# Expert tiles in the order in which they fill, with the first weights fetched for each tile as TensorE's stationary operand, and a start phase with smaller plans

## The chip, the core and the metric

The kernel is one program on one core of a Trainium2 chip. The metric is the device time of one execution in microseconds (us). Three executions of the kernel before took 6120.17, 6154.52 and 6066.71 us, median 6120.17. Five engines run side by side, each with its own instruction stream, and meet only through semaphores: TensorE (PE, with its weight loads shown as PEld), VectorE (DVE), ScalarE (ACT), GpSimd (POOL) and SyncE (SP). A name with a q behind it (SPq, POOLq) is the engine's instruction queue, where DMAs are issued.

## What is computed

The reference is one layer of a graph network followed by a mixture of experts, for 6250 nodes of 256 numbers and 200000 edges.

```
h   = gat(layernorm(x), W1, 4 heads);  h = elu(h);  g = gat(h, W2, 1 head)
      # gat: h = x @ W; per edge e = leaky_relu(s[src] + d[dst]); softmax of e over
      # the edges of one dst (self loops added); out[dst] = sum of weight * h[src]; + b
x   = x + g
n   = layernorm(x)
p   = softmax(n @ gate_w + gate_b)          # 8 experts
top2_vals, top2_idx = top_k(p, 2)
out = x + sum over the two experts e of a node:
          p_e * (gelu(n @ W1[e] + b1[e]) @ W2[e] + b2[e])    # 256 -> 512 -> 256
```

Everything is float32.

## The kernel before

`build` runs the phases one behind the other, with a barrier between two of them. The 6250 nodes are NT = 49 tiles of 128.

1. `start_phase` (0 to 139 us) normalizes the 49 node tiles, multiplies each with W1 (and the attention vectors folded into it) and stores a table of rows in DRAM. Beside this it plans the edges: it counts how many windows of 128 edges fall to each node tile, ranks the tiles by that (`rank_tiles`), gives each item its tile (`place_items`), and brings 13 blocks of source and destination indices in. On DVE all this stands between the normalizing steps of the tiles, at fixed tile numbers (`COUNT_AT`, `RANK_AT`, `ITEMS_AT`, `BLOCK_AT`). ACT first issues the loads of the weights and twelve small loads of attention columns (L624), then takes part in the tiles.
2. `shift_phase` and `edge_phase`, once for each of the two graph layers. In `edge_phase` POOL gathers eight times 128 source rows per step (L1002), ACT and DVE make the weights, PE sums rows with a 0/1 matrix (L1149), and DVE adds the sums (L1257). In `shift_phase` POOL issues the first 16 gathers (L694) while DVE prepares bounds and multiplies all of `acc` with the weights `ws` of the self loops (L818).
3. `route_phase` (5394 to 5556): SP loads all weights of all experts into SBUF (L1480, L1481; W1 4 MB, W2 4 MB, biases 3 MB in copies for all partitions). DVE finds the two best experts of each node and a slot in a list sorted by expert. The list has SLOT_TILES = 106 tiles of 128 slots; each expert's part is filled up to whole tiles. POOL then scatters the 49 tiles of rows twice (L1502) into the DRAM list `sent`, all first choices and then all second ones; between the two, DVE writes the new home number into the rows (L1581), for which it waits until the first 49 scatters have landed.
4. `expert_phase` (from 5564) walks over the 106 tiles k in the order of the list. SP loads `xe` (L1622, two buffers). PE transposes it (`turn_x`, L1668), ACT copies it to SBUF (L1781), PE multiplies with W1 (`up`, L1678: x is the stationary operand, 512 columns of W1 move), DVE adds b1 (L1729), ACT applies gelu (L1785), PE transposes the four pieces of the result (`turn_h`, L1687), DVE copies them (L1736), PE multiplies with W2 (`down`, L1697), DVE adds b2 (L1743), POOL scatters the result into `back` (L1651). The order on PE is written out by hand: in step k stand up(k+1), turn_x(k+2), turn_h(k), down(k-1). SP's load of tile k waits until tile k-2 is transposed and its home numbers are read (L1620, L1621). The first expert tile begins when all scatters have landed.
5. `combine_phase` (from 6018) reads the two results of each node back (L1819), weighs and adds them.

A float32 matmul appears in the trace as two passes, each with a weight load. `steps(eng, count, body, ways, peeled)` writes out the first and last steps and puts a loop around the others.

## Time and profile before

| | us |
|---|---|
| median of 3 executions (lowest, highest) | 6120.17 (6066.71, 6154.52) |
| the profiled execution, its own time | 6092.53 |
| span of its trace | 6090.7 |
| busy: PE / DVE / POOL / ACT | 3576.1 / 3420.2 / 3368.1 / 1636.8 |
| start phase, until the first shift phase | 139 |
| the two edge phases | 2589 + 2594 |
| routing up to the first scatter, the scatters | 28, 134 |
| expert stage, combining | 462, 73 |

The profile is of one execution, so every duration below comes from it; its own time is 27.6 us under the median. Engine rows give the start, the busy time, the engine, the line of kernel.py and what is written from what; a bracket gives the idle time of the engine before it and what ended it. The granted clock (PEclk) is given as a share of TensorE's 2.4 GHz; 0.50 is the lower of its two levels, 1.2 GHz.

### The profile page before, as it was taken

To read this page: it belongs to the slowest core of one execution; us is meant where nothing else is said; L and a number is where in the kernel's file an instruction comes from. 1 tells how busy PE (TensorE), PEld (TensorE's weight loads), DVE (VectorE), ACT (ScalarE), POOL (GpSimd) and SP (SyncE) were. 2 spreads that over 40 slices of the span, in tenths; PEclk is the share of its full clock that TensorE was granted. 3 is DMA by queue.
4 is the path that set the end of the run, shared out by engine and by line. 5 is a ranking of instruction groups with operands and counts; after the bars stand their busy time and mean duration, and the time that the engine had idled before them with its cause. 6 is when DMAs were issued, how large, how long until landed. Compare 5 with 4: busy or idle time off the path is not lost. (4 is left out here: it accounts for less than half of the span.)

```text
span 6090.7 us, 75071 instructions
## 1 busy us (share of the span) xinstructions
PE 3576.1 (59%) x12549; PEld 2299.2 (38%) x12550; DVE 3420.2 (56%) x8873; ACT 1636.8 (27%) x3595; POOL 3368.1 (55%) x3575
## 2 busy tenths in 40 slices
PE   5455555565555555554556666566666656624994
PEld 3233333333333333332333333333333333312773
DVE  7555555555555555555555555555555555531444
ACT  3222222222222222221233332322233333311222
POOL 4655555555555555555555555555655555644222
PEclk8666667766777777776676666666666676667997
DMA  4344444444444444443444444444444444442224
GB/s 127 104 109 108 105 108 110 109 107 106 109 108 109 110 110 110 110 104 86 111 114 114 115 114 114 113 114 114 114 113 114 114 113 114 118 137 86 91 64 155
DMA packets 321285, 670.43 MB, mean 110 GB/s; under 512 B 76855, under 2 KB 152773, under 8 KB 320938
## 3 DMA queue, kind: packets, MB, share of 16 engines
q0 software_dynamic: 170848, 469.37, 29.3%
q1 hardware_dynamic: 148585, 199.90, 11.5%
q10 hardware_dynamic: 1792, 0.53, 0.0%
q8 instruction: 18, 0.29, 0.0%
q14 instruction: 42, 0.34, 0.0%
HBM read 602.38 MB, written 75.12 MB: 111 GB/s over the span
## 5 line engine op out<-in xcount | busy, mean ns | idle before, releaser
L1002 POOL DMA_INDIRECT rows<-table,idx x3200 | 3031.4, 947 | 2086.8 <-issue 925.9
L1149 PE MATMUL bank<-rows,hit 128*128 128x260 f32 (+1 forms) x6464 | 2655.5, 553 | 2049.4 <-DVE acc L1257 1033.4
L1149 PEld LDWEIGHTS bank<-rows,hit 128*128 128x128 f32 x6464 | 1538.6, 265 | 2916.4 <-issue 1406.1
L1257 DVE TENSOR_TENSOR acc<-acc,bank 128x260 f32 (+1 forms) x3232 | 1356.4, 420 | 1385.5 <-remote 569.6
L1032 ACT ACTIVATE arg<-arg 128x32 f32<-128x32 f32 (+1 forms) x404 | 88.4, 219 | 3415.3 <-DVE arg L1237 2364.4
L1244 DVE TENSOR_TENSOR rows<-rows,bank 128x1024 f32<-128x1024 f32 x808 | 946.0, 1212 | 11.1 <-issue 9.7
L1211 DVE TENSOR_TENSOR hit<-bank,dst_loc 128x256 f32<-128x256 f32 x1616 | 671.7, 417 | 69.9 <-issue 58.6
L1222 DVE TENSOR_REDUCE bank<-bank 128x64 f32<-128x192 f32 (+1 forms) x404 | 115.4, 286 | 667.5 <-remote 598.8
L1026 ACT ACTIVATE hit_t<-gap,ones 128x1024 bf16<-128x1024 bf16 x404 | 463.8, 1148 | 20.3
L1021 ACT ACTIVATE gap<-loc,minus_node 128x1024 bf16<-128x1024 bf16 x404 | 462.6, 1145 | 11.7 <-DMA loc<-loc_row 11.5
L1138 PE MATMUL bank<-du,hit_t 128*128 x3232 | 340.9, 182 | 129.9 <-issue 127.6
L1138 PEld LDWEIGHTS bank<-du,hit_t 128*128 128x128 bf16 x3232 | 271.4, 102 | 332.2 <-issue 245.6
L1651 POOL DMA_INDIRECT back<-ye,xe_home x106 | 101.9, 962 | 341.3 <-DVE xe_home L1752 336.2
L1678 PE MATMUL bank<-fw,xet 128*128 x424 | 200.7, 596 | 0.9 <-ACT xet L1781 0.8
L1697 PE MATMUL bank<-fw,hidt 128*128 x848 | 200.5, 379 | 0.0
L1781 ACT COPY xet<-bank 128x256 f32<-128x256 f32 x106 | 39.5, 373 | 461.9 <-PE bank L1668 461.9
L1697 PEld LDWEIGHTS bank<-fw,hidt 128*128 128x128 f32 x848 | 152.9, 190 | 16.7 <-issue 0.2
L1729 DVE TENSOR_TENSOR hid<-bank,fb 128x512 f32<-128x512 f32 x106 | 73.3, 691 | 119.9 <-PE bank L1678 119.9
L1668 PE MATMUL bank<-ident,xe 128*128 128x128 f32 x212 | 41.1, 276 | 155.5 <-DMA xe<-sent 155.5
L1502 POOL DMA_INDIRECT sent<-acc,slot x98 | 96.2, 982 | 60.2 <-issue 29.3
L1743 DVE TENSOR_TENSOR ye<-bank,fb 128x256 f32<-128x256 f32 x106 | 45.0, 424 | 123.6 <-PE bank L1697 123.6
L1668 PEld LDWEIGHTS bank<-ident,xe 128*128 128x128 f32 x212 | 29.9, 142 | 211.9 <-issue 211.1
(223 smaller groups left out, 2191.9 us busy)
## 6 DMA issues: line engine op xcount, KB each, us to landing
loc<-loc_row SPq DMA_DIRECT2D x404, 256.0 KB
rows<-table,idx POOLq DMA_INDIRECT x3200
sent<-zeros SPq DMA_DIRECT2D x202, 68.3 KB
xe<-sent SPq DMA_DIRECT2D x106, 128.5 KB
got<-back SPq DMA_DIRECT2D x96, 128.0 KB, 3.4
fw<-in_L_ffn_W SPq DMA_DIRECT2D x16, 512.0 KB, 9.0
table<-acc POOLq DMA_DIRECT2D x49, 130.0 KB
table<-acc SPq DMA_DIRECT2D x49, 128.5 KB
```

The source lines that it names most:

```text
L1002: pool.indirect_dma_start(rows[:, way, n, 0:R], None, table, bass.IndirectOffsetOnAxis(idx[:, way, n:n + 1], 0)).then_inc(rows_in[way], 16)
L1021: nc.scalar.activation(gap[:, :], loc[:, way % 2, :], ACT.Abs, bias=kp.minus_node[:, 0:1]).then_inc(gap_ready, 1)
L1026: nc.scalar.activation(hit_t[:, way % 2, :, :].rearrange("p n e -> p (n e)"), gap[:, :], ACT.Relu, bias=kp.ones[:, 0:1], scale=-1.0).then_ ...
L1138: last = nc.tensor.matmul(du_bank[:, n * 6 * H:(n + 1) * 6 * H], hit_t[:, way % 2, n, :], eb.du3[:, t, :, 0:2 * H], start=True, stop=True)
L1149: nc.tensor.matmul(sum_bank[n % 4][:, 0:R], hit[:, way, n, :], rows[:, way, n, 0:R], start=True, stop=True).then_inc(summed, 1)
L1211: nc.vector.tensor_tensor(hit[:, way, some, :], col.unsqueeze(1).to_broadcast([P, PAIR, P]), eb.dst_loc[:, bass.ds(s * ST + pair * PAIR, P ...
L1222: nc.vector.tensor_reduce(du_edge, spread_out, AX.X, ALU.add).then_inc(du_kept, 1)
L1244: nc.vector.tensor_tensor(r, r, weight[:, some, :].unsqueeze(3).to_broadcast([P, PIECE, H, D // H]), ALU.mult).then_inc(scaled, 1)
L1257: nc.vector.tensor_tensor(kp.acc[:, t, 0:R], kp.acc[:, t, 0:R], sum_bank[n % 4][:, 0:R], ALU.add).then_inc(added, 1)
L1651: pool.indirect_dma_start(kp.back, bass.IndirectOffsetOnAxis(home[:, way:way + 1], 0), ye[:, way % 2, :], None).then_inc(y_out[way % 2], 16)
L1678: last = nc.tensor.matmul(kp.bank[2 + j][:, :], xet[:, j, c * P:(c + 1) * P], fb.w1[:, e, c, :], start=(c == 0), stop=(c == 1))
L1697: last = nc.tensor.matmul(kp.bank[6 + j][:, 0:D], hidt[:, j, c * P:(c + 1) * P], fb.w2[:, e, c, :], start=(c == 0), stop=(c == HC - 1))
```

## The change

The change rewrites the start and everything behind the edge phases, which it leaves as they are.

**Experts.** `route_phase` and `expert_phase` become one block without a barrier between them.
- The tiles are worked in the order in which they fill up while the node tiles are sent. DVE computes for each list tile the node tile that completes it, ranks these keys (two small products on PE), and writes a table of expert numbers and first rows, `table_of`.
- POOL sends first and second choices in turns (the second one three tiles behind, behind a wait for the first one's landing), eight pairs ahead, and then one pair before each second result scatter. SP's load of tile k waits for the second send of node tile (k + 7) // 2.
- W2 stays resident. W1 does not: SP fetches W1 of the tile's expert, 512 KB, into one of four slots, two tiles ahead. The fetch waits until gelu has freed the slot.
- `up` uses W1 as stationary operand (8 products of 128 columns of x), so that the result comes out transposed. The four transposes, DVE's bias and DVE's copy go; gelu reads PSUM in four pieces with the bias as a column per partition, which DVE picks out (`pick_bias`).
- On PE step k is turn_x(k+2), up(k+1), down(k).

**Shift phases.** `ws` is in a PSUM bank instead of SBUF; the product over `acc` is the same.

**Start.** x is loaded in pairs of tiles with eight buffers; the attention vectors come as four loads of rows and are transposed by PE; ranking works on 49 partitions with rows of 49 instead of 128 partitions with 2401; items are placed with small products on PE; the addition of eps moves into ACT's square root; constants of the later phases are made here.

The diff, cut:

```diff
@@ build @@
-            fb.w1 = fb.sb("fw1", [P, EXPERTS, 2, HID], F32)
...
@@ start_phase @@
-    COUNT_AT, RANK_AT, ITEMS_AT = 2, 4, 6
-    BLOCK_AT = [8 + 3 * blk for blk in range(BLOCKS)]
+    TURN_2, COPY_2, FOLD_2, KEEP_2 = 1, 2, 3, 4
+    COUNT_AT, RANK_AT, ITEMS_AT = 3, 5, 9
+    BLOCK_AT = [12 + 35 * blk // 12 for blk in range(BLOCKS)]
+    XSETS = 8
...
-                    done.then_wait(tt(less[:, :, :], key[:, :].unsqueeze(1).to_broadcast([P, NT, NT]),
-                                      key[:, :].unsqueeze(2).to_broadcast([P, NT, NT]), ALU.is_lt))
+                    done.then_wait(ts(less[:, 0, :], key[:, 0:NT], key[:, NT:NT + 1], None, ALU.is_lt))
+                    done.then_wait(tt(less[:, 1, :], less[:, 0, :], length[:, 0:NT], ALU.mult))
...
+                    done.then_wait(ts(past[:, :], item_row[:, :], end[:, :], None, ALU.is_ge))
+                    nc.vector.scalar_tensor_tensor(within[:, :], item_row[:, :], rank[:, 1:2], past[:, :],
+                                                   ALU.is_ge, ALU.subtract).then_inc(within_ready, 1)
...
+                    for m, a in enumerate((a_src, a_dst)):
+                        act.dma_start(vec[n][m * H:(m + 1) * H, :], a).then_inc(att_in[n], 16)
@@ shift_phase @@
-        ws = b.sb(f"ws_{layer}", [P, NT, HEADS], F32)
+        ws = kp.bank[2][:, 0:NT * HEADS].rearrange("p (t h) -> p t h", t=NT)
@@ expert_phase, SP @@
+                def load_weights(k, way):
+                    e = sp.value_load(fb.table_of[0:1, bass.ds(k, 1)], min_val=0, max_val=X - 1)
+                    if not number(k) or k >= RING:
+                        sp.wait_ge(gelu_ready, (k - RING + 1) * HC)
+                    sp.dma_start(w1[:, way % RING, :, :], fw1[bass.ds(e, 1)].rearrange("o (c p) n -> p (o c) n", p=P)
+                                 ).then_inc(w1_in[way % RING], 16)
+
+                def load(k, way, turn):
+                    if not number(k) or k + 2 < T:
+                        load_weights(k + 2, way + 2)
+                    j, after = way % 2, (way + 7) // 2
+                    row = sp.value_load(fb.table_of[0:1, bass.ds(k + T, 1)], min_val=0, max_val=(T - 1) * P)
+                    if not early(k):
+                        sp.wait_ge(x_turned, k - 1)
+                        sp.wait_ge(home_ready, k - 1)
+                    if not number(k) or turn * 4 + after < NT:
+                        sp.wait_ge(second_sent[after % 4], (turn + after // 4 + 1) * 16)
+                    sp.dma_start(xe[:, j, :], kp.sent[bass.ds(row, P), :]).then_inc(x_in[j], 16)
...
@@ expert_phase, POOL @@
+                def send_second(t):
+                    few = LAST if t == NT - 1 else P
+                    pool.wait_ge(first_sent[t % SENDS], 16 * (t // SENDS + 1))
+                    nc.gpsimd.iota(kp.acc[:, t, D:D + 1], [[0, 1]], base=(SLOT_TILES + NT + t) * P, channel_multiplier=1,
+                                   allow_small_or_imprecise_dtypes=True).then_inc(home_moved, 1)
...
+                for t in range(SENDS):
+                    send_first(t)
+                for t in range(FIRST):
+                    send(t)
+                for k in range(T):
+                    if k % 2 == 0:
+                        send(k // 2 + FIRST)
+                    store(k)
@@ expert_phase, PE @@
+                def up(k, way, turn):
+                    j = way % 2
+                    pe.wait_ge(w1_in[way], (turn + 1) * 16)
+                    pe.wait_ge(xet_ready, k + 1)
+                    if not early(k):
+                        pe.wait_ge(gelu_ready, (k - 1) * HC)
+                    for h in range(HC):
+                        for c in range(2):
+                            last = nc.tensor.matmul(kp.bank[2 + j][:, h * P:(h + 1) * P],
+                                                    w1[:, way, c, h * P:(h + 1) * P], xet[:, j, c * P:(c + 1) * P],
+                                                    start=(c == 0), stop=(c == 1))
+                    last.then_inc(up_done, 1)
...
+                def step(k, way, turn):
+                    j = way % 2
+                    if not number(k) or k + 2 < T:
+                        turn_x(k + 2, j, turn * 2 + way // 2 + 1)
+                    if not number(k) or k + 1 < T:
+                        up(k + 1, (way + 1) % RING, turn + (way + 1) // RING)
+                    down(k, way, turn)
@@ expert_phase, ACT @@
-                def gelu(k, j):
-                    act.wait_ge(hid_ready, k + 1)
-                    nc.scalar.activation(hid[:, j, :], hid[:, j, :], ACT.Gelu).then_inc(gelu_ready, 1)
+                def gelu(k, way):
+                    j = way % 2
+                    act.wait_ge(up_done, k + 1)
+                    act.wait_ge(bias_ready, k + 1)
...
+                    for h in range(HC):
+                        nc.scalar.activation(hidt[:, j, h * P:(h + 1) * P], kp.bank[2 + j][:, h * P:(h + 1) * P],
+                                             ACT.Gelu, bias=b1_now[:, way, h:h + 1]).then_inc(gelu_ready, 1)
```

How the instructions move is shown at two places. The first is SP in the loop over expert tiles. Before, two tiles of the loop, with `xe` the rows of the tile and `acc<-mid_x` a load for the combining (ISA rows are waits and register work):

```order
L1622 ISA
L1622 DMA xe<-sent 128x257
L1626 ISA
L1626 DMA acc<-mid_x 128x256
L1622 ISA
L1622 DMA xe<-sent 128x257
```

Now, one tile of the loop on SP, where `w_now` is the slot of W1 and `expert_and_row_of` the table of tiles:

```order
L1599 TENSOR_LOAD expert_and_row_of
L1599 ISA x2
L1601 ISA
L1602 ISA
L1602 DMA w_now<-in_L_ffn_W 128x2x512
L1609 ISA
L1609 TENSOR_LOAD expert_and_row_of
L1609 ISA x2
L1614 ISA
L1615 ISA
L1615 DMA xe<-sent 128x257
```

What moved: ahead of each `xe` load there now stand a fetch of W1 with its own wait (L1601) and a second register load from the table (L1609).

The second place is PE in the same loop. Before, one step, with the up products (`fw,xet`), the transposes of x and of the hidden tile (`ident,hid`), and the down products (`fw,hidt`):

```order
L1678 ISA
L1678 MATMUL bank<-fw,xet 128x512
L1678 ISA
L1678 MATMUL bank<-fw,xet 128x512
L1668 MATMUL bank<-ident,xe 128x128 x2
L1687 MATMUL bank<-ident,hid 128x128 x4
L1661 ISA
L1661 TENSOR_LOAD expert_of
L1661 ISA x2
L1697 ISA
L1697 MATMUL bank<-fw,hidt 128x256
```

Now, one step on PE up to its first down product:

```order
L1696 MATMUL bank<-ident,xe 128x128 x2
L1703 REGISTER_ALU
L1705 REGISTER_ALU
L1708 MATMUL bank<-xet,w_now 128x128 x8
L1689 REGISTER_ALU
L1689 TENSOR_LOAD expert_and_row_of
L1689 ISA x2
L1719 REGISTER_ALU
L1720 ISA
L1720 MATMUL bank<-fw,hidt 128x256
```

What moved: the transposes of x stand at the head of the step, ahead of the up products of the tile before; these are eight of 128 columns instead of two of 512; and the four transposes of the hidden tile are gone.

## Rows read from the trace of the kernel before

**Rows 1.** Busy by stage: stretch, length, PE, PEld, DVE, ACT, POOL, clock, DMA, GB/s.
```profile
174.00:2763.00 2589.00, 1509.58 (x5130) 959.79 (x5130) 1499.13 (x3825) 680.18 (x1543) 1515.80 (x1600) 0.71 0.41 108
...
5394.00:5422.00 28.00, 2.98 (x4) 1.17 (x4) 20.30 (x48) 1.81 (x2) 1.97 (x5) 0.50 0.99 364
...
5556.00:6018.00 462.00, 437.76 (x1908) 306.88 (x1908) 195.33 (x424) 107.52 (x213) 102.16 (x107) 0.97 0.24 74
```

**Rows 2.** Timeline of one tile of the expert stage.
```profile
5702.23 1.88 PE L1678 MATMUL bank<-fw,xet 128*128 x4
...
5702.98 0.20 DVE L1752 TENSOR_SCALAR xe_home<-xe,spare_home 128x1 int32<-128x1 f32 x1
...
5703.42 0.33 SPq L1622 DMA_DIRECT2D xe<-sent  x1
...
5703.95 0.38 PE L1668 MATMUL bank<-ident,xe 128*128 128x128 f32 x2
...
5704.16 0.60 PE L1687 MATMUL bank<-ident,hid 128*128 128x128 f32 x4
5704.27 0.69 DVE L1729 TENSOR_TENSOR hid<-bank,fb 128x512 f32<-128x512 f32 x1 [1.09 <-PE bank L1678]
...
5704.60 1.89 PE L1697 MATMUL bank<-fw,hidt 128*128 x8
...
5706.33 1.02 PE L1678 MATMUL bank<-fw,xet 128*128 x2
```

**Rows 3.** Timeline of the scatters, the first expert tile and the stage's end.
```profile
5420.64 1.72 POOL L1502 DMA_INDIRECT sent<-acc,slot  x1 [25.86 <-DVE slot L1573]
...
5482.18 1.57 POOL L1502 DMA_INDIRECT sent<-acc,slot  x1 [0.30 <-issue]
5488.36 0.21 DVE L1581 TENSOR_SCALAR acc<-home 128x49 f32<-128x49 f32 x1 [65.15 <-DMA sent<-acc,slot]
...
5564.39 0.33 SPq L1622 DMA_DIRECT2D xe<-sent  x1
...
5566.54 0.21 DVE L1752 TENSOR_SCALAR xe_home<-xe,spare_home 128x1 int32<-128x1 f32 x1 [77.97 <-DMA xe<-sent]
...
6018.60 0.81 SPq L1819 DMA_DIRECT2D got<-back  x2
```

**Rows 4.** Timeline of ACT: 128x128 pieces from PSUM with a bias column.
```profile
2759.09 0.37 ACT L1045 ACTIVATE tile_neg<-bank,minus_b 128x128 f32<-128x128 f32 x1 [5.71 <-PE bank L1158]
2759.35 0.33 ACT L1047 ACTIVATE bank<-bank,b_column 128x128 f32<-128x128 f32 x1
```

**Rows 5.** Lines L1480 and L932 on SP: ns min/median/max; and landing of weight loads.
```profile
L932 SPq TENSOR_LOAD <-tile_order x147: 6/657/838, 366.0 to 5375.8; - x147
...
L1480 SPq DMA_DIRECT2D fw<-in_L_ffn_W x8: 428/1730/1842, 5394.6 to 5408.2; - x8
...
DMA to landing us min/median/max: 4.0/9.0/9.8
```

**Rows 6.** Timeline of PE in the edge phase, behind idle gaps.
```profile
1505.50 0.71 PE L1149 MATMUL bank<-rows,hit 128*128 128x260 f32 x2 [2.79 <-issue]
...
1564.30 1.24 PE L1149 MATMUL bank<-rows,hit 128*128 128x260 f32 x2 [3.60 <-issue]
```

**Rows 7.** Timeline of PE at the head of the expert stage.
```profile
5568.50 5.09 PE L1678 MATMUL bank<-fw,xet 128*128 x8 [0.16 <-issue]
```

**Rows 8.** Timeline of the start phase: ACT's first root, and ranking.
```profile
10.71 1.28 ACT L592 ACT_TABLE_LOAD   x1 [10.58 <-issue]
...
31.62 2.66 DVE L430 TENSOR_TENSOR less<-key 128x2401 f32<-128x2401 f32 x1
```

**Rows 9.** Timeline of DVE and POOL in a shift phase and in an edge phase.
```profile
149.41 13.76 POOL L694 DMA_INDIRECT rows<-table,src_idx  x1 [0.30 <-issue]
...
183.95 2.35 DVE L1244 TENSOR_TENSOR rows<-rows,bank 128x1024 f32<-128x1024 f32 x2 [0.68 <-issue]
184.27 0.94 POOL L1002 DMA_INDIRECT rows<-table,idx  x1 [0.33 <-issue]
```

More of the change, by code:

```diff
@@ L119, in build @@
         keep.minus_node = k("minus_node", [P, 1], F32)
+        keep.node = k("node", [P, 1], F32)
+        keep.node_rows = k("node_rows", [P, 1], F32)
+        keep.down = k("countdown", [P, EXPERTS], F32)
+        keep.lower = k("lower", [P, P], F32)
+        keep.home = k("home", [P, NT], F32)
+        keep.spare = k("spare_home", [P, SLOT_TILES], F32)
         keep.bank = [ctx.enter_context(nc.psum_tensor(f"bank{n}", [P, 512], F32)) for n in range(8)]
@@ L349, in _ @@
                              ).then_inc(windows_written, 16)
+                for t in range(SETS, XSETS):
+                    load(t)
                 sp.wait_ge(pads_ready, 2)
@@ L437, in rank_tiles @@
-                    done.then_wait(tt(off[:, :], start[:, :], begin[:, :], ALU.subtract))
-                    same = less[0:1, :, :]
-                    done.then_wait(tt(same, rank[0:1, :].unsqueeze(1).to_broadcast([1, NT, NT]),
-                                      kp.col[0:1, 0:NT].unsqueeze(2).to_broadcast([1, NT, NT]), ALU.is_equal))
-                    done.then_wait(tt(same, same, kp.col[0:1, 0:NT].unsqueeze(1).to_broadcast([1, NT, NT]), ALU.mult))
-                    done.then_wait(nc.vector.tensor_reduce(order_f[:, :], same, AX.X, ALU.add))
@@ new lines, in load_mid, with load_both @@
+                def load_mid(t):
+                    sp.dma_start(kp.acc[:, t, 0:D], kp.mid[bass.ds(t * P, P), :]).then_inc(mid_in, 16)
+                def load_both(k, way, turn):
+                    load(k, way, turn)
+                    if way % 2 == 1:
+                        load_mid(turn * 4 + way // 2)
+                sp.wait_ge(table_ready, 1)
+                load_weights(0, 0)
+                load_weights(1, 1)
+                for t in range(3):
+                    sp.wait_ge(second_sent[t], 16)
@@ L1485, in _ @@
+                turns = (NT - 4) // 4
+                for k in range(8):
+                    load_both(k, k, 0)
+                with sp.Fori(1, turns) as turn:
+                    for way in range(8):
+                        load_both(turn * 8 + way, way, turn)
+                for k in range(turns * 8, T):
+                    load(k, k % 8, k // 8)
+                    if k - turns * 4 < NT:
+                        load_mid(k - turns * 4)
+                sp.wait_ge(mid_in, 16 * NT)
             @block.gpsimd
@@ new lines, in down @@
+                def down(k, way, turn):
+                    j = way % 2
+                    e = expert(k)
+                    if not early(k):
+                        pe.wait_ge(y_ready, k - 1)
+                    for h in range(HC):
+                        pe.wait_ge(gelu_ready, k * HC + h + 1)
+                        last = nc.tensor.matmul(kp.bank[6 + j][:, 0:D], hidt[:, j, h * P:(h + 1) * P],
+                                                fb.w2[:, e, h, :], start=(h == 0), stop=(h == HC - 1))
+                    last.then_inc(down_done, 1)
@@ L1520, in _, with expert, pick_bias @@
+                steps(pe, T, step, RING)
             @block.vector
             def _(dve):
+                def expert(k):
+                    return dve.value_load(fb.table_of[0:1, bass.ds(k, 1)], min_val=0, max_val=EXPERTS - 1)
+                def pick_bias(k, way):
+                    e = expert(k)
+                    if not number(k) or k >= RING:
+                        dve.wait_ge(gelu_ready, (k - RING + 1) * HC)
+                    nc.vector.tensor_copy(b1_now[:, way, :], b1_all[:, e, :]).then_inc(bias_ready, 1)
@@ new lines, in bias_y, with find_home @@
+                def bias_y(k, j, pair):
+                    e = expert(k)
+                    dve.wait_ge(down_done, k + 1)
+                    if not early(k):
+                        dve.wait_ge(y_out[j], pair * 16)
+                    nc.vector.tensor_tensor(ye[:, j, :], kp.bank[6 + j][:, 0:D], fb.b2[:, e, :], ALU.add
+                                            ).then_inc(y_ready, 1)
+                def find_home(k, way, turn):
+                    j, pair = way % 2, turn * 2 + way // 2
+                    dve.wait_ge(x_in[j], (pair + 1) * 16)
+                    if not number(k) or k >= RING:
+                        dve.wait_ge(y_out[j], (pair - 1) * 16)
+                    nc.vector.tensor_scalar(home[:, way:way + 1], xe[:, j, D:D + 1],
+                                            kp.spare[:, k:k + 1] if number(k) else kp.spare[:, bass.ds(k, 1)], None, ALU.max
+                                            ).then_inc(home_ready, 1)
```

621 lines of the change are left out of this document (316 added, 305 removed).

## The prediction, made before the changed kernel ran

> **What bounds the kernel now.** I read the page first, then the busy time by stage, then the waits and single tiles of the stages that the diff touches. The stages [rows 1] show that some 5,180 us of the 6,090.7 us span are the two edge phases (one from 174 to 2763 in the rows, its like from 2800 to 5394). The diff leaves their instructions alone, so I move them by nothing. What it touches is the start and the two shift phases (139 us, and some 35 each, by the table above) and all from 5394 on: 28 us of routing, 134 us in which only POOL works, 462 us of experts, 73 us of combining.
>
> In the expert stage TensorE is busy 437.8 us of 462 at a granted clock of 0.97 [rows 1]. One tile [rows 2] runs from the up matmuls at 5702.23 to the next at 5706.33, 4.10 us, with no idle PE row between: 1.72 us up (to 5703.95), 0.21 for two transposes of x, 0.44 for four of the hidden tile, 1.73 down. The bound is PE, and the xe load is issued at 5703.42 for a tile that PE turns two steps later, so its latency is hidden. Between the first scatter at 5420.64 and the landing of the first xe at 5566.54 lie 145.9 us [rows 3], in which POOL issues 98 scatters: 48 of them in the 61.5 us to 5482.18, 1.28 us each, a wait for the landing of that half, and the other half.
>
> **The expert loop, part by part.** The change feeds w1 as stationary operand: 8 products of 128 columns (16 passes) in place of 2 of 512 (4 passes). The number of columns is the same, and the four transposes and DVE's bias and copy go. The small transposes, each with a weight load of its own, start 0.11 us apart (0.44 / 4 [rows 2]), so 16 passes are 16 x 0.11 = 1.76 us. Were a weight load of 0.16 us on the average (306.88 / 1908 [rows 1]) not hidden, they would be 16 x 0.16 more at worst, 4.3 in all; but down starts its 8 passes 0.22 apart (1.73 / 8) with a load for each, so loads are hidden, and I take 1.76. PE's work per tile falls to 0.21 + 1.76 + 1.73 = 3.70 us. That alone would give back 0.40 x 106 = 42 us.
>
> But the loads change more. In SP's new order the load of tile k stands behind the w1 fetch for tile k+2, and that fetch waits until the gelu of tile k-2 has freed its slot. Gelu of k-2 follows up of k-2; and up of k-2 stands, in PE's order, behind the transposes of tile k-1. So there is a ring with one tile per round: x of tile k-1 lands, it is turned, up(k-2), gelu(k-2), w1 fetch, x of tile k is issued and lands. The two xe buffers don't help, since issue waits for nearly the latest work. The price of a round at full clock:
> - transposes of x: 0.21 us [rows 2].
> - up until ACT starts: 1.76, and 0.32 more, since DVE starts its bias at 5704.27, 2.04 after an up that streams for 1.72 [rows 2]. Together 2.08.
> - gelu, four pieces of 128x128 from PSUM with a bias column: the nearest rows start 0.26 apart and last 0.37 [rows 4], so 3 x 0.26 + 0.37 = 1.15.
> - to SP: DVE ends at 5703.18, SP issues at 5703.42, 0.24 [rows 2].
> - w1 fetch and xe load: the xe load needs, after the 0.43 us issue of a 512 KB fetch, a register load (0.66, median) [rows 5] and the 2.15 us from issue to landing of the first load (5564.39 to 5566.54 [rows 3]). From below: 3.24 us. From above: a 512 KB weight load took at least 4.0 us to land [rows 5], and the 128.5 KB behind it another 0.36 at the 364 GB/s of the routing stage [rows 1]: 4.36. I take 4.06, nearer to the upper end, since both go on SP's one queue and the register work around the load has its cost too.
>
> The round is 0.21 + 2.08 + 1.15 + 0.24 + 4.06 = 7.74 us, of which PE works 3.70 and waits 4.04. By the Trainium skill (DMA: Bandwidth & Descriptors, Queues, rings and completion order) each DMA engine takes a queue's descriptors in ring order, which speaks for the upper end; by it the last term is 4.36 and the round 8.04. No row of the kernel before shows such a pair.
>
> **The clock.** With such waits TensorE falls to its lower level. In the edge phase two passes take 0.71 us after an idle gap of 2.79 us and 1.24 after one of 3.60 [rows 6], which is 2.4 and 1.2 GHz. After a gap of 4.04, longer than both, I expect most rounds to begin at 1.2 GHz. A round whose transposes and up run wholly at 1.2 costs 0.21 + 1.76 = 1.97 more, 9.71 us. In a burst of work the higher level comes back before its end: the first 8 passes of the expert stage took 5.09 us [rows 7], between 8 x 0.43 = 3.4 at the higher level and 6.8 at the lower. So part of an up may be fast, and some rounds start fast: I take two thirds of 1.97, 1.3, and a round of 9.0 us. By the Trainium skill (TensorE: Matmul & The Clock Gate, HAM oscillation) a loop whose every burst waits for a DMA starts every burst throttled; by that rule the round is 9.71, which is a rival below.
>
> **The sends.** They are now interleaved: three first sends, then pairs of a second and a first, and SP lets tile 0 go when the fourth second send has landed. 3 x 1.28 + 4 pairs of about 3.0 (2 x 1.28, an iota, two waits) = 15.8 us, less the last first send (1.3), plus 4.6 for landing (the last scatter of the first half ends its issue at 5483.75, DVE answers at 5488.36 [rows 3]), plus 1.0 and 2.15 to xe: about 23 us after the first scatter, in place of 145.9. So 123 us come back here. The new table of tiles (some 20 DVE operations of 0.2 to 0.6 us and two trips to PE, about 9 us) lies beside these 23 us; if it didn't, it would cost 9. The remaining sends, 4 POOL DMAs per two tiles or 5.5 us, fit into two rounds of 18.
>
> **The stage's sum.** First xe at 5420.6 + 23 = 5443.6. Tiles 2 to 103 are 102 rounds of 9.0 = 918. The other four need no w1 fetch ahead of their load, 4 x 3.7 = 15. Filling and draining take today 6018.6 - 5566.5 less 106 x 4.10 = 17 [rows 2, 3], and I keep that. Combining starts at 6393.6 in place of 6018.6: +375 us.
>
> **The other parts.** Start: seven DVE operations of 2.66 us on 2401 columns, 18.6 in all, stall every engine from 31.62 on [rows 8]; the new form works on 49 partitions with rows of 49 (0.2 us each) and two of 1664 columns (1.8 us each by 2.66 x 1664 / 2401), 6 us in all: -13. Placing items has seven operations on 637 columns (0.7 us each by the same rule) and is left with four small ones: -5. ACT's 12 attention loads end at 10.7, before the first root [rows 8]; now four, done by about 5: -6. One DVE operation less per tile, 49 x 0.1: -5. Together -29, bounds -15 and -45, since POOL's stores may bound the rest; I take -30. Shift: while DVE's product of `acc` runs, one of POOL's gathers takes 13.76 us; beside a product with an operand in PSUM (L1244) a gather takes 0.94 [rows 9]. With ws in PSUM the 16 gathers no longer stand still; DVE's product is late next, so that of 13 us some 9 come back, twice: -18, bounds 0 and -26. Routing's weight loads shrink by 4 MB beside DVE's chain: nothing. Combining: the same work, nothing.
>
> **The sum.** +375 - 30 - 18 = +327 on a span of 6090.7 is 6417.7, with 1.8 us around it 6419.5. The median of the three runs before is 6120.2, 27.7 above this profiled execution; I add a third of that and say 6430 us, 5% slower.
>
> **Rivals.** With a round of p us the whole is 5501.5 + 102p by these sums (5443.6 + 102p + 32, less 6018.6, less 48, plus 6092.5).
> - *The clock stays high*: p = 7.74, 6291 us. For it: the stage's 3.7 us bursts are denser than the edge phase's. Against it: 4.04 is longer than the gap of 3.60, behind which the level was low [rows 6].
> - *Every round starts low*: p = 9.71, 6492 us. For it: the low level behind a gap of 3.60 [rows 6]. Against it: the 5.09 us for the first 8 passes [rows 7], in which the level rose within the second up. This is the case in which the rule of the Trainium skill's TensorE page, named above, would come out.
> - *The ring doesn't bind, not slower*: the xe load lands while PE is still at work, so that PE's 3.7 us are the round. Then 5501.5 + 102 x 3.75 = 5884 us, 3.4% faster. For it: today's load hides fully [rows 2], and the sends' 123 us are a sure gain. It decides from p = 5.8 down (5501.5 + 592 = 6093); so from the gelu's end to x's landing only 2.36 us might pass, where the landing alone takes 2.15 and a register load 0.66 lies ahead of it.
> - *A short ring*: the lower end of each term, p = 6.7 (3.24 for the loads, full clock, and 0.1 less at up and at gelu), 5501.5 + 683 = 6185 us, within 2%. For it: the 2.15 us of a load that stands alone [rows 3]. Against it: the 512 KB ahead on the same queue.
>
> **How the numbers follow.** Forecast (mixed clock) 0.50, clock high 0.20, every round low 0.19, short ring 0.08, ring not binding 0.03. A measurement of this kernel tells about 2% (122 us) from no change; the whole is more than that above 6092.5 from p = 7.0 on. So slower 0.89, same 0.08, faster 0.03. The range takes the cases of high and low clock in: 6250 (p = 7.35) to 6530 (p = 9.9, with 20 us for the spread of the runs).
>
> **What would show it.** Right: in the expert stage PE waits once per tile for the DMA of xe, about 4 us, before the transposes; SP waits for gelu; the clock there is 0.6 to 0.8; xe lands some 2.5 us or more after its own issue; the first expert tile starts about 23 us after the first scatter; the start is some 105 to 115 us long, and a shift phase about 26. Wrong: PE rows back to back in that stage, or a round under 7.0 us; a wait for second sends or for POOL in place of that for xe; or edge phases that differ by more than their spread.

## The result

The changed kernel takes 6496.3 us (median of 4 executions, 6440.0 to 6520.7), the kernel before 6113.9 (median of 4, 6066.7 to 6154.5). The ratio is 1.0615, with a 95% interval of 1.051 to 1.072: slower by 6%. The forecast was 6430 us, in a range of 6250 to 6530. The profiled execution has a span of 6482.5 us and a time of its own of 6484.6.

### The profile page after: what moved, and what is told of

The parts are those of the page before. It is cut to its first block and busy times, and to the rows that moved or that the text cites. A ratio compares the mean times of both kernels' runs of the same rounds, so it can differ in the third digit from the quotient of the medians.

```text
span 6482.5 us, 77188 instructions
## 1 busy us (share of the span) xinstructions
PE 3685.8 (57%) x13440; PEld 2475.2 (38%) x13441; DVE 3286.2 (51%) x8728; ACT 1696.3 (26%) x3913; POOL 3344.6 (52%) x3631
## 3 DMA queue, kind: packets, MB, share of 16 engines
q1 hardware_dynamic: 174761, 249.21, 13.1%
## 5 line engine op out<-in xcount | busy, mean ns | idle before, releaser
L1224 PE MATMUL bank<-rows,hit 128*128 128x260 f32 (+1 forms) x6464 | 2606.4, 544 | 2109.1 <-issue 1239.4
L1224 PEld LDWEIGHTS bank<-rows,hit 128*128 128x128 f32 x6464 | 1496.5, 260 | 2978.2 <-issue 1735.9
L1101 ACT ACTIVATE hit_t<-gap,ones 128x1024 bf16<-128x1024 bf16 x404 | 463.8, 1148 | 20.2
L1213 PE MATMUL bank<-du,hit_t 128*128 x3232 | 361.1, 181 | 111.3 <-issue 78.1
L1708 PE MATMUL bank<-xet,w_now 128*128 128x128 f32 x1696 | 338.8, 384 | 0.0
L1708 PEld LDWEIGHTS bank<-xet,w_now 128*128 128x128 f32 x1696 | 325.2, 295 | 3.3 <-issue 0.6
L1696 PE MATMUL bank<-ident,xe 128*128 128x128 f32 x212 | 57.7, 363 | 416.3 <-DMA xe<-sent 402.9
L1720 PE MATMUL bank<-fw,hidt 128*128 x848 | 230.1, 420 | 0.0
L1900 ACT ACTIVATE hidt<-bank,b_now 128x128 f32<-128x128 f32 x424 | 120.9, 368 | 280.4 <-PE bank L1708 277.4
L1720 PEld LDWEIGHTS bank<-fw,hidt 128*128 128x128 f32 x848 | 180.7, 225 | 24.5
## 6 DMA issues: line engine op xcount, KB each, us to landing
xe<-sent SPq DMA_DIRECT2D x106, 128.5 KB
table<-acc SPq DMA_DIRECT2D x49, 128.5 KB
```

Source lines behind the costliest of these rows:

```text
L1101: nc.scalar.activation(hit_t[:, way % 2, :, :].rearrange("p n e -> p (n e)"), gap[:, :], ACT.Relu, bias=kp.ones[:, 0:1], scale=-1.0).then_ ...
L1213: last = nc.tensor.matmul(du_bank[:, n * 6 * H:(n + 1) * 6 * H], hit_t[:, way % 2, n, :], eb.du3[:, t, :, 0:2 * H], start=True, stop=True)
L1224: nc.tensor.matmul(sum_bank[n % 4][:, 0:R], hit[:, way, n, :], rows[:, way, n, 0:R], start=True, stop=True).then_inc(summed, 1)
L1708: last = nc.tensor.matmul(kp.bank[2 + j][:, h * P:(h + 1) * P], w1[:, way, c, h * P:(h + 1) * P], xet[:, j, c * P:(c + 1) * P], start=(c = ...
L1720: last = nc.tensor.matmul(kp.bank[6 + j][:, 0:D], hidt[:, j, h * P:(h + 1) * P], fb.w2[:, e, h, :], start=(h == 0), stop=(h == HC - 1))
L1900: nc.scalar.activation(hidt[:, j, h * P:(h + 1) * P], kp.bank[2 + j][:, h * P:(h + 1) * P], ACT.Gelu, bias=b1_now[:, way, h:h + 1]).then_i ...
```

## The profile after

The first view is the busy time by stage, with the columns of [rows 1]: stretch and its length, then busy time and instructions of PE, PEld, DVE, ACT and POOL, the granted clock, DMA share and GB/s. The stretches are the first shift phase, the two edge phases, routing up to the first scatter, the sends up to the first x on PE, and the expert stage until PE ends.

```profile
109.03:134.22 25.19, 0.97 (x3) 0.58 (x3) 21.70 (x27) 1.65 (x3) 15.30 (x16) 0.50 0.32 85
134.22:2746.64 2612.42, 1492.07 (x5142) 928.97 (x5142) 1510.52 (x3836) 682.59 (x1553) 1512.20 (x1600) 0.70 0.41 107
2769.73:5362.93 2593.20, 1517.88 (x5142) 962.11 (x5142) 1520.83 (x4080) 771.25 (x1550) 1512.50 (x1600) 0.69 0.42 112
5362.93:5390.18 27.25, 2.98 (x4) 1.17 (x4) 19.42 (x51) 1.81 (x2) 0.00 (x0) 0.56 0.55 193
5390.18:5410.42 20.24, 1.86 (x6) 0.70 (x6) 4.96 (x20) 0.00 (x0) 15.75 (x23) 0.50 0.52 177
5410.42:6404.60 994.18, 588.44 (x2756) 518.78 (x2756) 77.06 (x316) 161.60 (x531) 188.46 (x230) 0.81 0.31 100
```

The answer to [rows 1] is in the last row: the expert stage has grown from some 460 us to 994, PE is busy in 59% of it instead of 95%, and the granted clock fell from 0.97 to 0.81. By the starts of the first instruction in each stage the two profiled executions differ like this (us):

| stage | before | after | difference | predicted |
|---|---|---|---|---|
| start | 137.4 | 109.0 | -28.4 | -30 |
| shift phases | 36.2 + 36.2 | 25.2 + 23.1 | -24.1 | -18 |
| edge phases | 2602.5 + 2582.0 | 2612.5 + 2593.2 | +21.2 | 0 |
| routing up to the first scatter | 26.5 | 27.2 | +0.8 | 0 |
| first scatter to first x on PE | 145.9 | 20.2 | -125.7 | -123 |
| from there until combining | 452.0 | 1000.7 | +548.7 | +498 |
| combining | 72.1 | 71.4 | -0.7 | 0 |

(The last prediction but one is +375 + 123. The first instruction of the first shift phase starts at 137.4; the 139 us given above for the start before are 1.6 too long.) One round of the expert stage, 9.82 us long and so a little over the mean, answers to [rows 2] in the timeline (start, busy time, engine, line, operation, in brackets the idle time before and what ended it):

```profile
5902.96 0.69 PE L1696 MATMUL bank<-ident,xe 128*128 128x128 f32 x2 [2.90 <-DMA xe<-sent]
5903.44 3.16 PE L1708 MATMUL bank<-xet,w_now 128*128 128x128 f32 x16
...
5906.44 1.89 PE L1720 MATMUL bank<-fw,hidt 128*128 x8
5906.64 1.14 ACT L1900 ACTIVATE hidt<-bank,b_now 128x128 f32<-128x128 f32 x4 [2.58 <-PE bank L1708]
5907.95 0.38 SPq L1602 DMA_DIRECT2D w_now<-in_L_ffn_W  x1
...
5909.24 0.33 SPq L1615 DMA_DIRECT2D xe<-sent  x1
...
5912.78 0.47 PE L1696 MATMUL bank<-ident,xe 128*128 128x128 f32 x1 [4.45 <-DMA xe<-sent]
```

Read it as a ring: x is turned, up follows, gelu ends at 5907.78, SP issues the w1 fetch 0.17 us later and the xe load 1.29 behind that, and 3.54 us after its issue PE turns that x. Down has ended at 5908.33, so PE then waits 4.45 us. The waits of the stage (total, number, longest), PE's and then those on SP's queue, show this for nearly every one of the 106 tiles (PE before x 104 times, 3.9 us each):

```profile
DVE ye L1772 <- PE bank L1720: 844.4, 106, 15.2
POOL back L1670 <- DVE xe_home L1781: 768.1, 103, 14.1
ACT xet L1891 <- PE bank L1696: 467.1, 90, 6.1
PE bank L1696 <- DMA xe<-sent: 402.9, 104, 7.1
```
```profile
SPq L1602 <- ACT hidt L1900: 684.5, 102, 9.9
SPq L1612 <- DVE xe_home L1781: 7.1, 1, 7.1
```

SP waits for gelu 102 times and hardly ever for anything else; POOL and DVE wait longer than PE, but only because PE's results come late. From the third turning of x to the 104th (5425.37 to 6382.80) it is 101 rounds of 9.48 us. Nearly all signs that the prediction names as right have come: a wait for x once a tile, SP behind gelu, 20 us to the first tile. The clock, 0.81, is just above its 0.6 to 0.8. Of its signs of being wrong, only the longer edge phases can be meant, and they come up again below.

In the first shift phase (DVE's product over `acc` and three of POOL's gathers, answering to [rows 9]) no gather stands still any more:

```profile
120.47 13.21 DVE L893 TENSOR_TENSOR acc<-acc,bank 128x12544 f32<-128x12544 f32 x1
```
```profile
119.83 0.94 POOL L769 DMA_INDIRECT rows<-table,src_idx  x1 [0.30 <-issue]
121.07 0.94 POOL L769 DMA_INDIRECT rows<-table,src_idx  x1 [0.30 <-issue]
```

## Experiments on the ring

Each kernel is the changed kernel with the edit shown. Where the round is split, "to gelu" is from PE's turning of x to the start of gelu, "landing" from the issue of the xe load to PE's turning of it; "to gelu" is a mean and the other parts are medians over the same 95 rounds in the middle of the stage. In the changed kernel the round is 3.66 to gelu + 1.14 for gelu + 0.17 to SP's fetch + 1.29 from fetch to xe issue + 3.23 landing, 9.49. (The expectations have 3.68, 3.22 and 3.02 for what is 3.66, 3.23 and 2.98 by the whole trace.)

The time of the same program differs between the chips on which it ran. `x_before_w1`, `eight_slots`, `wait_kept_x_first` and `gap_filled` ran on chip 1 and `half_fetch` on chip 4, where the kernel before takes about 6100 us. The other seven ran on chips 2 and 6, where it takes 4980, so their totals compare only with that; the last section comes to this. The expert stage of the kernel before is the same in both (452.0 and 452.9 us). All but `x_before_w1`, `eight_slots_four_x` and `front_alone` have a single execution and are read by their stages. How far one can trust these: the four kernels in which the ring is as in the changed one have expert stages of 995.0 to 1000.7 us.

**The order on SP.** 

> SP issues the xe load of tile k before the w1 fetch for tile k+2 instead of behind it; nothing else changes. Theory (a ring of one tile, closed by the order on SP's queue): the ring opens to two tiles. From the turning of x(k-2): 2.3 us to gelu at full clock, 1.15 gelu, 0.2 to SP, 1.3 to the xe issue, 3.1 landing, 8.0 us for two tiles, so 4.0 to 4.4 us a round in place of 9.48, TensorE's clock over 0.95 in the stage, 6484.6 - 101 x 5.2 = 5960 us (5920 to 6060), about 0.975 of the kernel before. Rival 1 (the 640 KB per tile themselves take the time, as transfers): a round stays over 6 us, 6130 us or more. Rival 2 (two xe buffers are too few): no change, 9.4 us, 6480 us.

```diff
 def load(k, way, turn):
-    if not number(k) or k + 2 < T:
-        load_weights(k + 2, way + 2)
...
     sp.dma_start(xe[:, j, :], kp.sent[bass.ds(row, P), :]).then_inc(x_in[j], 16)
+    if not number(k) or k + 2 < T:
+        load_weights(k + 2, way + 2)
```

6004.2 us against 6096.6, ratio 0.984 (0.983 to 0.986): the same instructions in another order beat the kernel before as well, by 1.6%. That is clear of the noise, though under the 2% from which this study calls a kernel faster. The round is 4.88 us on the average, the clock 0.95.

```profile
5399.14:5927.81 528.67, 432.46 (x2756) 383.16 (x2756) 77.03 (x316) 160.43 (x531) 192.22 (x235) 0.95 0.59 189
```
```profile
SPq L1602 <- ACT hidt L1900: 168.7, 62, 7.9
```

Bandwidth isn't the limit (189 GB/s where the changed kernel moved 100), nor are two xe buffers. The sum was 0.5 to 0.9 us too low. In the pair of rounds from 5602.16 to 5611.49 the parts are 3.02 to gelu, 1.14, 0.16, 2.44 from fetch issue to xe issue and 2.57 landing, 9.33 for two tiles: the mid_x load of every second tile stands between the fetch and the load, which the expectation left out. Gelu came 0.7 us late behind an up that shows its usual 1.96 us; the trace doesn't tell why.

**The wait.** 

> w1 and its bias get eight slots in place of four; the order on SP stays (fetch for k+2 ahead of the load of x(k)), and the fetch waits for a gelu four tiles older. Theory: the wait for gelu was what closed the ring, so this alone also opens it: 4.0 to 4.5 us a round, about 5960 us, although every x load still goes behind 512 KB. Rival (being behind the fetch on the queue costs the time, whatever it waits for): 7 us a round or more, over 6230 us. Rival (the wait isn't the cause): 9.4 us, 6480 us.

```diff
-    RING = 4
+    RING = 8
```

(The counts that go by pairs of tiles, `turn * 2`, become `turn * (RING // 2)`.) 5942.9 us, a round of 4.24, clock 0.98. The order is that of the changed kernel, every x still goes behind 512 KB, and the round has more than halved. So it is the wait ahead of the fetch, not the fetch, that closes the ring. SP's waits in the stage are now for home numbers, which DVE reads out of the xe buffer:

```profile
SPq L1614 <- DVE xe_home L1781: 63.5, 45, 4.5
SPq L1612 <- DVE xe_home L1781: 41.3, 30, 3.0
SPq L1602 <- ACT hidt L1900: 1.2, 4, 0.5
```

**The buffers.** 

> The changed kernel with four xe buffers in place of two (each load may go two tiles earlier as far as buffers go); four w1 slots and the order on SP as they are. Theory: issue waits for the fetch, and the fetch for gelu, so buffers change nothing: 9.4 to 9.6 us a round, 6460 to 6500 us. Rival (two xe buffers hold the loads back): a round of 5 us or less, under 6050 us.

```diff
+    XB = 4
...
-    xe = b.sb("xe", [P, 2, D + 1], F32)
+    xe = b.sb("xe", [P, XB, D + 1], F32)
...
-    if not early(k):
-        sp.wait_ge(x_turned, k - 1)
-        sp.wait_ge(home_ready, k - 1)
+    if not number(k) or k >= XB:
+        sp.wait_ge(x_turned, k - XB + 1)
+        sp.wait_ge(home_ready, k - XB + 1)
```

5353.5 us (before: 4983.3), a round of 9.50 us, an expert stage of 999.9 us: nothing, as the prediction said of the two buffers. (The total in the expectation was for a chip of the 6100 us kind.)

**Both.** 

> Eight w1 slots and four xe buffers together. With eight slots alone the mean round was 4.24 us: rounds of 3.8, in which TensorE doesn't wait, in turn with rounds of 4.2 to 5.6, in which x comes late, since SP waits for the home numbers of the tile two before. Theory: with four buffers that wait goes too and TensorE's own work is the round, 3.8 us: 5941 - 101 x 0.44 = 5897 us (5880 to 5925), about 0.967 of the kernel before. Rival (the DMA engines, busy 0.75 there, are the limit): 4.2 us stays, 5940 us.

The edit is that of the two runs above together.

4762.7 us against 4983.3, ratio 0.956 (0.954 to 0.957). The round is 3.74 us, PE's rows stand back to back. SP still waits 83 us in all for home numbers, but that costs nothing, since x is issued 10 us before its turning:

```profile
4500.83 0.38 PE L1698 MATMUL bank<-ident,xe 128*128 128x128 f32 x2
4501.05 1.95 PE L1710 MATMUL bank<-xet,w_now 128*128 128x128 f32 x16
4502.84 1.89 PE L1722 MATMUL bank<-fw,hidt 128*128 x8
4504.57 0.38 PE L1698 MATMUL bank<-ident,xe 128*128 128x128 f32 x2
```
```profile
4276.73:4687.34 410.61, 398.86 (x2756) 371.12 (x2756) 77.07 (x316) 161.87 (x531) 188.72 (x230) 0.98 0.78 241
```

This is the forecast's PE work of 3.70 us per tile, which the changed kernel had but could not show, and the fastest kernel of the study. DMA engines busy at 0.78 don't limit it; the rival fell. So the buffers for x are worth nothing while the wait for gelu closes the ring, and 0.50 us a round once it is open.

**The last term.** 

> Keeps the one-tile ring on purpose: SP reads both registers first, waits for the same gelu as in the changed kernel, and then issues x(k) and behind it the w1 fetch for k+2. It prices the last term of the ring, of which the trace shows 1.29 us from fetch issue to xe issue and about 3.1 from xe issue to the turning. Theory: the round loses the 1.29 us and, with nothing ahead on the queue, the landing falls to the 2.15 us of a lone load: 9.48 - 1.29 - 0.95 = 7.2 us, 6258 us (7.0 to 8.2 us, 6230 to 6355). Rival (the 512 KB ahead cost the landing nothing): 8.2 us, 6354 us. If the round fell under 5 us, the ring would not be closed by this wait at all.

```diff
-        load_weights(k + 2, way + 2)
+        e = sp.value_load(fb.table_of[0:1, bass.ds(k + 2, 1)], min_val=0, max_val=X - 1)
     row = sp.value_load(fb.table_of[0:1, bass.ds(k + T, 1)], min_val=0, max_val=(T - 1) * P)
+    sp.wait_ge(gelu_ready, (k + 2 - RING + 1) * HC)
...
     sp.dma_start(xe[:, j, :], kp.sent[bass.ds(row, P), :]).then_inc(x_in[j], 16)
+    sp.dma_start(w1[:, (way + 2) % RING, :, :], fw1[bass.ds(e, 1)].rearrange("o (c p) n -> p (o c) n", p=P)
+                 ).then_inc(w1_in[(way + 2) % RING], 16)
```

(Shown without the conditions for the first and last tiles.) 6199.8 us, a round of 6.64, which is below the expected 7.0 to 8.2. SP issues 0.18 us after gelu and PE turns x 2.14 after that, as a lone load did in [rows 3] (2.15):

```profile
5603.13 0.33 SPq L1618 DMA_DIRECT2D xe<-sent  x1
5603.65 0.38 SPq L1620 DMA_DIRECT2D w_now<-in_L_ffn_W  x1
...
5605.27 0.44 PE L1702 MATMUL bank<-ident,xe 128*128 128x128 f32 x2 [1.77 <-DMA xe<-sent]
```

So 1.29 + 1.09 = 2.38 us of the round are the price of the fetch ahead of the load (landing 2.14 instead of 3.23). The rest of the 2.84 us that went lies in "to gelu", 3.03 instead of 3.66, which the expectation had left as it was. An up takes 2.43 us on the average instead of 3.25, with 2.1 us of idle time ahead of the turning instead of 3.9, and 0.23 of that is lost again between the end of up and gelu.

**The size of the fetch.** 

> The changed kernel, but from the fifth tile on only the first half of W1's rows of the tile's expert is fetched (256 KB in place of 512); the other half of the slot keeps what an earlier tile left, so the up products use wrong weights for half of their rows. Instructions and waits are the same. It tells what the 1.07 us are made of that x needs longer behind a fetch (3.22 us from its issue) than alone (2.14). Theory (they are the time in which the 512 KB move): half of them go, x is turned 2.7 us after its issue, the round is 9.0 us, 50 us less in the expert stage. Rival (a fixed cost of having a fetch ahead on the queue): 3.2 us and a round of 9.45 stay. Rival (all of it hangs on the last 256 KB): 2.2 us, a round of 8.4 us.

```diff
+    n = 2 if number(k) and k < RING else 1
-    sp.dma_start(w1[:, way % RING, :, :], fw1[bass.ds(e, 1)].rearrange("o (c p) n -> p (o c) n", p=P)
+    sp.dma_start(w1[:, way % RING, 0:n, :], fw1[bass.ds(e, 1), 0:n * P].rearrange("o (c p) n -> p (o c) n", p=P)
```

6339.4 us (before: 6123.6), a round of 8.04, landing 2.31. Of the 1.09 us behind 512 KB, 0.92 go with half of it; the theory of a proportional share fell, and the second rival came nearest. One reading, only argued: 256 KB are nearly gone in the 1.25 us until xe is issued, so that only what is left of 512 KB stands in its way. The round fell by more than the landing, since to gelu it took 3.15 us instead of 3.66.

**The clock.** 

> The changed kernel with 20 more transposes of the identity into an unused bank behind each down (2.2 us at full clock), work whose result nobody reads; it lies in TensorE's gap of 3.9 us. It prices the clock term. Theory: the level stays high, transposes and up take 0.2 + 1.95 us in every round, and the round falls from 9.48 by the 1.2 us or so that are added by the low level: 8.2 us, 6355 us (6330 to 6400), clock over 0.95 in the stage. Rival (the low level isn't on the ring, or the extra work delays it): 9.4 us or more, 6480 us or more.

```diff
+    FILL = 20
...
     last.then_inc(down_done, 1)
+    for n in range(FILL):
+        nc.tensor.transpose(kp.bank[5][:, n % 4 * P:(n % 4 + 1) * P], kp.ident[:, :], kp.ident[:, :])
```

6435.2 us, a round of 8.86: half of what was expected. To gelu it took 2.98 us. TensorE was still idle for 1.9 us ahead of a turning, and 50 of the 106 ups were slow (over 2.5 us, where the others take at most 2.05; the 38 of 109 in the next expectation is a miscount). Hence a second dose, with the one edit:

```diff
-    FILL = 20
+    FILL = 34
```

> As gap_filled, with 34 transposes of the identity behind each down (3.8 us at full clock) in place of 20, so that only 0.2 to 0.4 us of the gap stay idle. With 20 the turning-to-gelu part was 3.02 us (3.68 without, 2.3 at full clock) and 38 of 109 ups were still slow. Theory: with hardly any idle time the level never falls, that part is 2.3 us and the round 9.48 - 1.4 = 8.1 us, clock over 0.97 in the stage. Rival (the extra work falls into x's way): 8.9 us or more again.

5233.5 us, a round of 8.28, 2.33 to gelu, and the rest nearly as it was (1.14, 0.17, 1.29, 3.35). TensorE is idle for 0.5 us ahead of a turning, at most 1.1, and 2 of 106 ups are slow. One round, and then the stages of the two:

```profile
4701.98 3.88 PE L1725 MATMUL bank<-ident 128*128 128x128 f32 x34
4706.68 0.44 PE L1697 MATMUL bank<-ident,xe 128*128 128x128 f32 x2 [0.83 <-DMA xe<-sent]
4706.97 2.05 PE L1709 MATMUL bank<-xet,w_now 128*128 128x128 f32 x16
```
```profile
5414.90:6360.90 946.00, 738.94 (x4876) 678.30 (x4876) 77.28 (x316) 161.59 (x531) 188.78 (x231) 0.90 0.32 105
```
```profile
4269.23:5158.51 889.28, 821.90 (x6360) 765.54 (x6360) 76.96 (x316) 161.57 (x531) 187.89 (x230) 0.99 0.35 111
```

PE does 3,604 more instructions and the stage, 889.3 us, is 111 shorter than the changed kernel's 1000.7. The low level thus costs 3.66 - 2.33 = 1.33 us a round (of which 1.25 in up). 8.28 is 0.2 over the theory, of which 0.12 is a later landing.

## Experiments on the other parts

**Start and shift phases alone.** 

> The kernel before with the start phase and the shift phases of the change (ws in PSUM), and its own routing, experts and combining. Theory: start -28 and shifts -24 by their stages, 52 us less than before, about 0.9915, if the edge phases keep their length of before. Rival (the edge phases get longer behind a shorter shift, as the rows after show, +10 and +11 us, and give it back): 25 to 35 us less, 0.995.

The edit puts `start_phase`, `shift_phase` and the constants that they make into the kernel before. 4927.2 us against 4983.3, ratio 0.989 (0.987 to 0.990), 56 us for the expected 52; like `x_before_w1`, clear of the noise and under 2%. Its stages beside the kernel before on the same chip: start 106.2 for 137.9, shift phases 25.2 and 23.1 for 36.1 and 36.1, edge phases 2031.2 and 2033.6 for 2036.4 and 2036.8. (The profiled execution, 4916.3 us, was 11 us shorter than the other three, so its stages show more than 56.) The edge phases did not get longer: that rival fell, at least on this chip.

**The shift phase by itself.** 

> The changed kernel with the shift phases of the kernel before (ws back in SBUF, product unchanged). Theory: one gather in each shift phase stands still for 13.8 us beside the product again, each phase is 36.2 us long in place of 25.2 and 23.1, 24 us more in all. Rival (the shorter shift phase came from something else in the new start): 25 and 23 us stay.

```diff
-        ws = kp.bank[2][:, 0:NT * HEADS].rearrange("p (t h) -> p t h", t=NT)
+        ws = b.sb(f"ws_{layer}", [P, NT, HEADS], F32)
```

The phases are 35.7 and 36.1 us long again, 23.5 us more in all for the expected 24, with one gather of 13.42 us in the first:

```profile
119.72 0.95 POOL L769 DMA_INDIRECT rows<-table,src_idx  x1 [0.30 <-issue]
120.97 13.42 POOL L769 DMA_INDIRECT rows<-table,src_idx  x1 [0.30 <-issue]
134.69 0.95 POOL L769 DMA_INDIRECT rows<-table,src_idx  x1 [0.30 <-issue]
```

Where one operand sits decides whether POOL's gathers go on beside a DVE product of 13.2 us. The Trainium skill (GPSIMD Engine Reference, Specifications) names contention with DVE instructions with two SBUF inputs. The traces agree: 13.42 us for the gather beside such a product, 0.94 with one input in PSUM.

**All sends first.** 

> The changed kernel, but POOL issues all 49 pairs of sends first and the first tile waits for all of them, as in the kernel before (which sent 98 rows of tiles without a wait for the first one's landing in each pair). Theory: 49 pairs of 2.69 us (seen in the trace after) less the 11 that stand ahead now, so first scatter to first x turned 20 + 38 x 2.69 + 3 = 125 to 140 us in place of 20, and nothing back in the expert stage, since the round waits for x: 110 to 120 us more. Rival (the sends lie on the ring of the expert stage, where POOL issues a pair every two tiles): the stage becomes shorter by 20 us or more.

```diff
-    FIRST = 8
+    FIRST = NT
...
-    for t in range(3):
-        sp.wait_ge(second_sent[t], 16)
+    for t in range(4):
+        sp.wait_ge(second_sent[t], 16 * ((NT - t + 3) // 4))
```

From the first scatter to the first x on PE it is 145.8 us again, 6 over the expected range, and the expert stage is 997.4 us long (999.9 in `four_x_alone`, 1000.7 in the changed kernel). The interleaving is worth 125 us, and nothing of note is paid back in the stage.

**The kernel before once more.** 

> The kernel before once more, for the lengths of its stages in a second execution. If the edge phases come out at 2602 and 2582 us within 3 us, the 10 to 23 us more that every kernel with the new front has shown in the first of them are an effect of the change; if they come out at 2610 or more, they are spread between executions.

4982.2 us, edge phases of 2036.4 and 2036.8 us. It could not tell what it was meant to, since it ran on chip 2. What can be said: on chips 2 and 6, six kernels with the new start have first edge phases of 2031 to 2035 us against 2036. Where the kernel before had 2602, six kernels have 2609 to 2625, among themselves 17 us apart, which the edits, all behind the edge phases, can't explain. The +21 us compare single executions out of sets in which one program's lie 81 and 88 us apart, so they may be spread. On chip 1, though, the four executions of `x_before_w1` lie within 4 us, and the four kernels profiled there have first edge phases 17 us apart. An estimate goes further. The other stages of the kernel before take 906 us in its trace, so that the medians of its spans on chips 1 and 4, 6094.8 and 6121.9, leave 5189 and 5216 for its two edge phases there. Four changed kernels on chip 1 are 6 to 22 us over that and `half_fetch` on chip 4 is 8 under. So the longer edge phases need not be an effect of the change; whether a part of them is, stays open.

## Why the prediction was right

- **What bounds it.** Right: a ring of one tile, closed by SP's order and the wait for gelu. `eight_slots` shows that the wait does it, `x_before_w1` that the order does, and `four_x_alone` that more buffers for x don't help while the ring is closed.
- **To gelu, at full clock** 0.21 + 2.08 = 2.29: measured 2.33 (`gap_filled_more`). **Gelu** 1.15: measured 1.14. **To SP** 0.24: 0.17.
- **Fetch and load, 4.06: too low.** This is the step that failed, a term that was sized too small. It measured 1.29 + 3.23 = 4.52, over the upper bound of 4.36 as well. The bound added a row's 0.36 us for 128.5 KB to a fetch that lands in 4.0; the load in fact takes 2.14 alone and 1.09 more behind the fetch, after 1.29 for issue and register load. The rule of the Trainium skill on ring order (DMA: Bandwidth & Descriptors, Queues, rings and completion order) pointed to the right end: x does wait for what is ahead of it.
- **The clock, 1.3 of 1.97.** Measured 1.33. The two thirds were chosen and not worked out, so that they fit this well is luck; the picture behind them is right. In the changed kernel 93 of the 106 ups are slow, 2.66 to 3.68 us, the other 13 take at most 2.05, and only 28 take 3.6 or more, as an up does that runs at the low level to its end. So nearly every round starts low, and in most the level rises before the up is done. The rule of the Trainium skill (TensorE: Matmul & The Clock Gate, HAM oscillation), that such bursts start throttled, comes out for 93 of 106; what it doesn't give is the 9.71 us of the rival "every round starts low", which had the whole up at the low level.
- **The round** of 9.0 measured 9.48, and 101 x 0.48 = 49 us are nearly the whole difference in the stage (+548.7 for +498). By its number alone 9.48 lies nearer to the rival of 9.71 than to 9.0; it is the parts that tell them apart, since 0.46 of the 0.48 us are the fetch and the load and next to nothing is clock.
- **Sends** -123: -125.7 (the terms add up to 22.3 us and not to 23; measured 20.2). **Start** -30: -28.4, in part by errors that cancel. ACT's first table load came 3.5 us earlier (7.21 for 10.71) and not 6, while the DVE operation that went from each tile was worth 7.5 us of DVE time in all and not 5. No run took the prices apart. **Shift** -18: -24.1. The term assumed that DVE's product would be late next and keep 4 us of each 13; it ends at 133.7 us, and the next phase starts 0.5 us later, so it does bound the phase, yet 11.0 and 13.1 came back.
- **Edge phases** 0: +21.2, see above. Together: +51 in the expert stage, +21 in the edge phases and -6 in the shift phases are the 65 us between +327 and +392, within 1.

Against the medians the forecast was 66 us low, about as much. The prediction held because its mechanism was right and its misses, 51, 21 and -6 us, are small beside the 392; that the 21 us of the edge phases, which it had at nothing, still fit into the range is no merit of its working.

## What to carry to other kernels

A prefetch that waits for a buffer must not stand on the queue ahead of a load that is needed at once: write down for each queue what the head waits for, and follow that wait round to the engine it feeds. Here one swapped pair of lines turned 6% slower into 1.6% shorter than before, and twice the slots with four xe buffers into 4.4% faster (220 us, on a chip where the kernel before takes 4983). Count the clock into any gap that is opened, since it put 1.3 us on top of 3.9 of idle time here, and read a smaller PE sum only as a bound, which shows when nothing else closes a ring.

## What was unexpected of the hardware

The same program took different times on different chips: about 6097 us on chip 1 and 6124 on chip 4, but 4983 on chip 2 and 4977 on chip 6. The first executions, 6067 to 6155 us, have no chip on record. The edge phases make nearly the whole difference (2602.5 and 2582.0 against 2036.4 and 2036.8 us). Groups of the page, kernel before in the first executions and on chip 2, the line of POOL's gathers (busy, mean ns, then the idle time before them):

```profile
L1002 POOL DMA_INDIRECT rows<-table,idx x3200 | 3031.4, 947 | 2086.8 <-issue 925.9
```
```profile
L1002 POOL DMA_INDIRECT rows<-table,idx x3200 | 3032.6, 948 | 985.2 <-issue 925.8
```

A gather takes 947 or 948 ns in both. On chip 2 POOL issues them 1.25 us apart almost without a gap (1600 x 1.25 = 2000 of 2036 us); in the first executions it waits another 1,100 us in all. Most of that is put down to the matmuls that sum the gathered rows (L1149). Here are these waits in the first edge phase, first executions and then chip 2:

```profile
POOL rows L1002 <- PE bank L1149: 461.4, 129, 8.3
```
```profile
POOL rows L1002 <- PE bank L1149: 33.7, 106, 1.7
```

So in the longer executions the buffers for rows come free later. What makes PE late there, and what differs between the chips, was not found. Start, shift phases, routing, sends, experts and combining of the kernel before agree within 1 us. Totals from different chips can therefore not be compared, but those stages can.

The share of slow ups follows the idle time ahead of a burst, but roughly. Over the same 95 rounds as above, 86 ups are slow with 3.9 us of idle time on the average (changed kernel), 64 with 2.9 (`half_fetch`), 33 with 2.1 (`wait_kept_x_first`), 46 with 1.9 and 20 more transposes (`gap_filled`), none with 0.5 and 34 of them (`gap_filled_more`). In `gap_filled` no idle time ahead of a turning was over 2.93 us in these rounds, and 46 of 95 ups were slow all the same. So the low level shows here behind gaps well under the 3.60 us of [rows 6], and the gap just ahead doesn't decide it by itself.
